# A state-space scan on one core: turned sums two units behind, and some inputs made by TensorE

## The reference, cut to what matters

```
x, z   = split(h @ in_proj)                  # 512 channels each
xc     = silu(conv4(x) + conv_b)             # 4 taps along time, per channel
dt, Bm, Cm = split(xc @ x_proj)              # 16 states
dt     = softplus(dt @ dt_proj + dt_b)
h[t]   = exp(dt[t] * A) * h[t-1] + dt[t] * xc[t] * Bm[t]    # per channel and state
y[t]   = sum over states of h[t] * Cm[t]
out    = ((y + D * xc) * silu(z)) @ out_proj
```

## Time and profile before

| | |
|---|---|
| median of 3 runs | 2810.18 us (2809.4 to 2818.44) |
| the profiled execution | 2800.64 us, span 2798.8 us |
| busy: TensorE, VectorE, ScalarE, GpSimd | 2379.9, 2118.9, 1563.2, 1135.3 us (85, 76, 56, 41%) |
| TensorE's granted clock, mean | 0.916 |
| stage A | 0 to about 520 us, scans from 44.76 us on |
| stage B | about 1515 to 2030 us |
| chain that ended last, by engine | TensorE 42%, VectorE 25%, ScalarE 11%, GpSimd 9% |

### The profile page before, as it was taken

One profiled execution on the slowest core, in us unless ns is written; L12 is line 12 of the kernel. 1 busy time (PEld: TensorE's weight loads), 2 busy tenths in 40 slices (PEclk: granted clock), 3 DMA queues, 4 the chain that ended last, 5 costly groups with the idle time before them and its releaser, 6 DMA issues.

```text
span 2798.8 us, 32693 instructions
## 1 busy us (share of the span) xinstructions
PE 2379.9 (85%) x11300; PEld 1600.5 (57%) x11300; DVE 2118.9 (76%) x3100; ACT 1563.2 (56%) x2734; POOL 1135.3 (41%) x829
## 2 busy tenths in 40 slices
PE   5989896689998798958995798897778987899998
PEld 2333432467776687847884234333333444799998
DVE  5999999699997365538894899999864653577776
ACT  6676574255665455516884866766313444266673
POOL 3889998200000444210221699989601134100004
PEclk9999999899999799979997899999867886799999
DMA  4032040570000000012421330303084231256553
GB/s 178 2 120 92 30 146 0 196 256 1 24 1 1 36 1 31 16 66 95 162 106 53 121 115 7 121 31 102 0 124 103 55 81 58 91 189 224 210 197 95
DMA packets 101607, 247.36 MB, mean 88 GB/s; under 512 B 9285, under 2 KB 65361, under 8 KB 94274
## 3 DMA queue, kind: packets, MB, share of 16 engines
q1 hardware_dynamic: 88530, 222.43, 24.6%
q0 software_dynamic: 5376, 14.70, 1.6%
q10 hardware_dynamic: 7536, 8.13, 1.2%
HBM read 187.96 MB, written 48.81 MB: 85 GB/s over the span
## 4 chain that ended last, share of the span: by engine, by line
PE 42%; DVE 25%; ACT 11%; issue 9%; POOL 9%; DMA 1%; SPq 1%; POOLq 1%; ACTq 1%; DVEq 0%
PE psum L111 7%; DVE psum L758 7%; PE psum L112 7%; PE psum L113 7%; PE psum L498 5%; POOL bu L372 4%; PE psum L118 3%; POOL ch L415 3%; ACT WH L3526 2%; ACT g L3673 2%; DVE ch L775 2%; PE psum L481 2%; DVE ch L758 2%; PE psum L2967 1%; PE psum L2895 1%
## 5 line engine op out<-in xcount | busy, mean ns | idle before, releaser
L372 POOL TENSOR_TENSOR bu<-u,row 128x1024 f32<-128x1024 f32 x254 | 594.8, 2354 | 137.0 <-DVE psum L758 47.5
L498 PE MATMUL psum<-ch,ident 128*128 128x512 f32 x1024 | 513.2, 634 | 114.6 <-DVE ch L775 63.7
L758 DVE TENSOR_TENSOR_SCAN psum<-psum,bu 128x1024 f32<-128x1024 f32 x210 | 479.8, 2285 | 22.1 <-ACT psum L590 21.2
L498 PEld LDWEIGHTS psum<-ch,ident 128*128 128x128 f32 x1024 | 190.4, 198 | 401.6 <-issue 184.1
L590 ACT ACTIVATE psum<-dt,A 128x511 f32<-128x511 f32 x512 | 332.1, 681 | 0.4
L775 DVE TENSOR_TENSOR ch<-psum,row 128x1024 f32<-128x1024 f32 x210 | 256.6, 1222 | 5.7
L3673 ACT ACTIVATE g<-psum,bias 128x256 f32<-128x256 f32 x248 | 101.1, 470 | 133.8 <-PE psum L113 129.6
L3495 POOL DMA_INDIRECT R<-m1res,gi x26 | 26.2, 1006 | 340.3 <-DMA m1res<-ob 324.2
L462 PE MATMUL psum<-hT,inw 128*128 128x512 f32 x256 | 130.0, 637 | 27.9 <-ACT xs L536 20.6
L111 PE MATMUL psum<-WH,hs 128*128 128x256 f32 x496 | 144.8, 292 | 5.0 <-DVE hs L3753 2.2
L111 PE MATMUL psum<-xT,WH 128*128 128x256 f32 x496 | 142.0, 286 | 7.6 <-DVE xT L3716 7.6
(11 more groups left out here) (456 smaller groups left out, 6536.7 us busy)
## 6 DMA issues: line engine op xcount, KB each, us to landing
W<-in_m1W SPq DMA_DIRECT2D x24, 2052.0 KB, 8.5
row<-Ascr SPq DMA_DIRECT2D x64, 512.0 KB, 5.7
...
```

Source lines behind the costliest of these rows:

```text
L372: e.tensor_tensor(m.bu[i % 3][:, :, :], u, m.row[:, g, 0, :, :], ALU.mult).then_inc(*m.fed.up)
L498: p = pe.matmul(m.y, k.ident, m.ch[i % RING_C][:, j, :], start=False, stop=g == UNITS - 1 and j == 1)
L758: dve.tensor_tensor_scan(to, flat, m.bu[i % 3][:, :, :].rearrange("p a n -> p (a n)"), 0.0, ALU.mult, ALU.add).then_inc(*m.scan.up)
```

## The change

TensorE's sum of unit i moves two slots later, to slot i + 2, and is made turned: each 128 x 128 block of h*C is the stationary operand and the identity moves, so y has time on the partitions. D*x is now a product of ScalarE (`mamba_direct_act`), turned into y in the same way. The gate is applied to turned y in unit 2 of a block, for which z is made with time on the partitions ("z by channel block"); the result is turned back by an item "yt" before the output projection. Unit 5 of every block gets its u*B from TensorE: u is turned (`mamba_turned_pe`), copied by ScalarE, and multiplied with diagonals of B which VectorE makes once per batch from an item "bt"; the decays of that unit go to an SBUF tile of their own. GpSimd makes the other seven, from three tiles counted over those units alone, and h*C of units 1, 3 and 5. Conv block 0 goes from GpSimd to TensorE. The slots of the items change, items of the batch ahead come before "out" in a slot, conv is drained in its own slot, the silu of z moves to slot 5 and that of xc to slot 16. The diagonals for conv are made in slots 8 and 9 of the first batch. Cut to its core:

```diff
+RING_B = 3
 RING_C = 4
 SIX = 6
+FROM_PE = (5,)
+BY_POOL = (1, 3)
...
-FIRST = [("h", 0), ("h", 1)] + [("in", i) for i in range(4)] + [("conv", 3), ("xp", 0)] + [("dt", i) for i in range(4)]
...
-BEFORE = {2: ("out", 0), 3: ("out", 1), 4: ("out", 2), 5: ("out", 3)}
-AHEAD = {6: ("h", 0), 7: ("h", 1), 8: ("in", 0), 9: ("in", 1), 11: ("in", 2), 12: ("in", 3),
-         14: ("conv", 1), 16: ("conv", 2), 18: ("conv", 3),
-         21: ("xp", 0), 22: ("dt", 0), 23: ("dt", 1), 24: ("dt", 2), 25: ("dt", 3),
-         26: ("z", 0), 28: ("z", 1), 29: ("z", 2), 30: ("z", 3)}
+FIRST = [("h", 0), ("h", 1)] + [("in", i) for i in range(4)] + [("conv", 3), ("xp", 0)] + [("dt", i) for i in range(4)] + [("bt", 0)]
...
+OPENING = {0: ("z", 0), 1: ("z", 1), 2: ("z", 2)}
+OWN = {3: ("z", 3), 13: ("yt", 0), 21: ("yt", 1), 28: ("yt", 2)}
+BEFORE = {4: ("yt", 3), 5: ("out", 0), 6: ("out", 1), 8: ("out", 2), 10: ("out", 3)}
+AHEAD = {6: ("h", 0), 7: ("h", 1), 8: ("in", 0), 9: ("in", 1), 10: ("in", 2), 11: ("in", 3),
+         12: ("conv", 0), 13: ("conv", 1), 14: ("conv", 2), 15: ("conv", 3),
+         17: ("xp", 0), 18: ("dt", 0), 19: ("dt", 1), 20: ("dt", 2), 22: ("dt", 3),
+         24: ("z", 0), 25: ("z", 1), 27: ("z", 2), 29: ("bt", 0)}
...
+    if s in OWN:
+        o.append((OWN[s][0], b, OWN[s][1]))
+    if b + 1 < B and s in AHEAD:
+        o.append((AHEAD[s][0], b + 1, AHEAD[s][1]))
     if b and s in BEFORE:
         o.append((BEFORE[s][0], b - 1, BEFORE[s][1]))
-    if b + 1 < B and s in AHEAD:
-        o.append((AHEAD[s][0], b + 1, AHEAD[s][1]))
...
-    b, n = i // PER, i % PER
-    return n % UNITS in (2, 5) and (b == B - 1 or n in (2, 5, 18, 21, 26))
+    return from_pe(i) or i % UNITS in BY_POOL
...
-            for j in range(2):
+            for j in (1,) if g in FROM_PE else range(2):
...
+def mamba_turned_pe(k, m, pe, i):
+
+    s = i // UNITS
+    pe.wait_ge(*m.u_in(s))
+    if i >= RING_A:
+        pe.wait_ge(*mamba_left(m, i - RING_A))
+    for c in range(4):
+        p = turn_in(k, pe, m.a[i % RING_A][:, 0, 128 * c:128 * c + 128], m.u[s % 2][:, 128 * c:128 * c + 128])
+    p.then_inc(*m.turned.up)
+
+
+def mamba_turned_act(k, m, act, s):
+    act.wait_ge(*m.turned(s))
+    act.copy(m.uT[:, :, :], m.a[(UNITS * s + FROM_PE[0]) % RING_A][:, 0, :].rearrange("p (c n) -> p c n", c=4)).then_inc(*m.uT_in.up)
+
+
+def mamba_input_pe(k, m, pe, i):
+
+    s, g = i // UNITS, i % UNITS
+    b, db = s // 4, s % 4
+    if g == FROM_PE[0]:
+        pe.wait_ge(*m.uT_in(s))
+    elif i >= RING_A:
+        pe.wait_ge(*mamba_left(m, i - RING_A))
+    if db == 0:
+        pe.wait_ge(*m.drawn(mamba_use("bt", b, 0)))
+    for j in range(2):
+        for c in range(4):
+            p = pe.matmul(m.a[i % RING_A][:, j, 128 * c:128 * c + 128], m.uT[:, c, :], m.diag_B[g][:, j, c, :], start=True, stop=True)
+    p.then_inc(*m.fed_pe.up)
...
+        if i + 2 < PER * B and not from_pe(i + 2):
             mamba_input(k, m, pool, i + 2)
         if by_pool(i):
             mamba_met_pool(k, m, pool, i)
-        if b + 1 < B and 9 <= n < 16:
-            mamba_conv_pool(k, m, pool, b + 1, n - 9)
...
-        if 28 <= n and b + 1 < B:
-            if n == 28:
+        if n == 0 and b:
+            mamba_dt(k, m, pool, 4 * b + 3)
+        if 29 <= n and b + 1 < B:
+            if n == 29:
...
+    elif w == "z":
+        for c in range(4):
+            for f in range(2):
+                p = pe.matmul(bank[:, 128 * c:128 * c + 128], m.hT[:, f, 128 * c:128 * c + 128], m.inw[:, f, T + 128 * j:T + 128 * j + 128],
+                              start=f == 0, stop=f == 1)
+    elif w == "yt":
+        pe.wait_ge(*m.gated(4 * b + j))
+        for c in range(4):
+            p = turn_in(k, pe, bank[:, 128 * c:128 * c + 128], m.yzT[:, c, :])
+    elif w == "bt":
+        pe.wait_ge(*m.drawn(mamba_use("xp", b, 0)))
+        W = R + 32
+        for c in range(4):
+            p = turn_in(k, pe, bank[:, W * c:W * c + W], m.xd[0:W, 128 * c:128 * c + 128])
...
-            p = pe.matmul(bank, m.dg[:, 4 * (j - 1) + f, :], m.xs[:, j, f:f + T], start=f == 0, stop=f == 3)
+            p = pe.matmul(bank, m.dg[:, 4 * (j - 1) + f, :] if j else m.dg0[:, f, :], m.xs[:, j, f:f + T], start=f == 0, stop=f == 3)
...
+def mamba_sum_pe(k, m, pe, i):
+
+    s, g = i // UNITS, i % UNITS
+    if g == 0:
+        if s:
+            pe.wait_ge(*m.gated(s - 1))
+        pe.wait_ge(*m.dx_in(s))
+        for c in range(4):
+            p = pe.matmul(m.y[:, c, :], m.dx[:, 128 * c:128 * c + 128], k.ident, start=c == 0, stop=False, is_transpose=True)
+        p.then_inc(*m.direct.up)
+    pe.wait_ge(*mamba_out(m, i))
+    for j in range(2):
+        for c in range(4):
+            p = pe.matmul(m.y[:, c, :], m.ch[i % RING_C][:, j, 128 * c:128 * c + 128], k.ident, start=False,
+                          stop=g == UNITS - 1 and j == 1 and c == 3, is_transpose=True)
+    p.then_inc(*m.summed.up)
...
-        s, g = i // UNITS, i % UNITS
+        if (i + 1) % UNITS == FROM_PE[0]:
+            mamba_input_pe(k, m, pe, i + 1)
         for item in mamba_items(i):
             mamba_item_pe(k, m, pe, *item)
-        if g == 0:
-            pe.wait_ge(*(m.gated(s - 1) if s else m.diag(1)))
-            pe.matmul(m.y, m.dg[:, 12 + s % 4, :], m.xc[:, s % SIX, :], start=True, stop=False).then_inc(*m.direct.up)
-        pe.wait_ge(*mamba_out(m, i))
-        for j in range(2):
-            p = pe.matmul(m.y, k.ident, m.ch[i % RING_C][:, j, :], start=False, stop=g == UNITS - 1 and j == 1)
-        p.then_inc(*m.summed.up)
+        if i >= 2:
+            mamba_sum_pe(k, m, pe, i - 2)
+        if (i + 2) % UNITS == FROM_PE[0]:
+            mamba_turned_pe(k, m, pe, i + 2)
+    for i in range(PER * B - 2, PER * B):
+        mamba_sum_pe(k, m, pe, i)
+    mamba_item_pe(k, m, pe, "yt", B - 1, 3)
...
+    elif w == "yt":
+        act.copy(m.yz[:, j, :], bank).then_inc(*m.drawn.up)
...
+        if b:
+            act.wait_ge(*m.gated(4 * (b - 1) + j))
+        act.copy(m.sz[:, j, :], bank).then_inc(*m.drawn.up)
...
-    for j in range(4):
-        z = m.sz[:, (4 * b + j) % SIX, :]
-        e = act.activation(z, z, ACT.Silu)
-    e.then_inc(*m.sz_in.up)
+    act.activation(m.sz[:, :, :], m.sz[:, :, :], ACT.Silu).then_inc(*m.sz_in.up)
+
+
+def mamba_direct_act(k, m, act, s):
+
+    act.wait_ge(*m.xc_in(s))
+    if s:
+        act.wait_ge(*m.direct(s - 1))
+    act.activation(m.dx[:, :], m.xc[:, s % SIX, :], ACT.Identity, scale=pv(k, m.L + "D", 4)[:, s % 4:s % 4 + 1]).then_inc(*m.dx_in.up)
...
+    if from_pe(i):
+        e = NTH[i]
+        if e:
+            act.wait_ge(*m.scan(FED_PE[e - 1]))
+        else:
+            act.wait_ge(*m.zeros(2))
+        a = m.ad[0]
+    else:
+        if i >= RING_A:
+            act.wait_ge(*mamba_left(m, i - RING_A))
+        a = m.a[i % RING_A]
+        act.copy(a[:, :, 0], m.zero[:, :])
...
+    mamba_direct_act(k, m, act, 0)
...
-
-        for item in mamba_items(i - 1) if i else []:
-            if item[0] == "conv":
-                mamba_item_act(k, m, act, *item)
+            if (i + 2) % UNITS == FROM_PE[0]:
+                mamba_turned_act(k, m, act, (i + 2) // UNITS)
         for item in mamba_items(i):
-            if item[0] != "conv":
-                mamba_item_act(k, m, act, *item)
+            mamba_item_act(k, m, act, *item)
...
-        if n == 6 and b:
+        if i in (8, 9):
+            for j in range(8) if i == 8 else range(4):
+                o, n0 = (m.dg, 4) if i == 8 else (m.dg0, 0)
+                g = act.activation(o[:, j, :], k.ident, ACT.Identity, scale=cw[:, n0 + j:n0 + j + 1])
+            g.then_inc(*m.diag.up)
+        if n == 14 and b:
             x_stats_act(k, act, 4 * (m.rnd + 1) + b - 1)
-        if n == (2 if b else 4):
+        if n == 5:
             mamba_gate_act(k, m, act, b)
-        if n == 5 and b + 1 < B:
+        if n == 4 and b + 1 < B:
             mamba_rows_act(k, m, act, b + 1)
-        if n == 19 and b + 1 < B:
+        if n % UNITS == 3 and i // UNITS + 1 < 4 * B:
+            mamba_direct_act(k, m, act, i // UNITS + 1)
+        if n == 16 and b + 1 < B:
             mamba_silu_act(k, m, act, b + 1)
-        if n in (24, 25) and b + 1 < B:
-            mamba_soft_exp_act(k, m, act, b + 1, 2 * (n - 24), 2 * (n - 24) + 2)
-        if n == 26 and b + 1 < B:
+        if n in (20, 22) and b + 1 < B:
+            mamba_soft_exp_act(k, m, act, b + 1, n - 20, n - 18)
+        if n == 23 and b + 1 < B:
             mamba_soft_log_act(k, m, act, 3 * b + 5, 0, 4)
...
-        if b:
-            dve.wait_ge(*m.full(mamba_use("out", b - 1, 3)))
-    dve.tensor_tensor(m.yz[:, db, :], m.y, m.sz[:, s % SIX, :], ALU.mult).then_inc(*m.gated.up)
+    if s:
+        dve.wait_ge(*m.full(mamba_use("yt", (s - 1) // 4, (s - 1) % 4)))
+    dve.tensor_tensor(m.yzT[:, :, :], m.y, m.sz[:, db, :].rearrange("p (c n) -> p c n", c=4), ALU.mult).then_inc(*m.gated.up)
...
+def mamba_diag_dve(k, m, dve, b, n):
+
...
```

(18 more changed lines are left out.)

134 lines of the change are left out of this document (64 added, 70 removed).

## The result

The changed kernel takes 2923.0 us (median of four runs, 2911.9 to 2928.7) against 2809.8: ratio 1.0392, interval 1.0354 to 1.0430. It is slower, as forecast, but by 113 us where 40 were forecast, and outside the range of 2785 to 2890.

A forecast was written before the change was run, and what follows sets the result against it. VectorE was taken to set the pace, GpSimd close behind. Per stage 6.2 + 10.7 + 10.4 - 6.5 - 0.4 = 20.4 us; two stages 40.8, rounded to +40 on 2810.2, gave 2850 us, range 2785 to 2890.

The forecast's parts named there:

- (a): Middle batch, units 3 to 8: VectorE waits 5.4 us for out1 behind h0, 0.4 for u*B; 6.0 with rounding.
- (b): Middle batch, units 8 to 13: out3, in3 and u*B of unit 13 come late, with the gate; 3.4 us.
- (c): Middle batch, units 13 to 21: serial conv, silu, xp, dt chain of 36.7 us against VectorE's 26.0; 10.6 us idle.
- (d): Middle batch, units 24 to 29: log delays a decay 2.2, gate waits 1.4, u*B of 29 0.3; 3.9 us.
- The first batch: First batch of a stage: first scan's wait for dt3 hidden by unit 2's decay; +6.2 us in all.
- The last batch: Last batch of a stage, nothing prepared ahead: 100.4 us to the last scan against 106.8; -6.5 us.
- the end: End of a stage: gate waits 1.1 us instead of 2.8, then a turned block and copy 1.3; -0.4 us.
- rival 3: TensorE's clock falls, slowing (c)'s matmuls: 2880 us if only early on, 2970 throughout; chance 0.10 shared with slow sums.
- the signs of being wrong: Middle batches under 112 us, VectorE's waits moving to GpSimd's inputs, or middle-batch clock below 0.9, blaming clock, not order.
- Rival 1: VectorE and GpSimd set the pace, ScalarE's chain being shorter: middle batches near 105, 2744 us; chance 0.20.
- a draw: Last-batch gains and partial stalls cancel: middle batch 116 to 118 us, total 2802 to 2818; chance 0.10.

The follow-up runs named there:

- the spread items: Changed kernel with the next batch's conv in slots 12, 14, 16, 18 and its later items moved along, to slot 30: 2874.0 us, ratio 1.0240.
- the pair of fillers: Plain or turned zero blocks before every sum, against the changed kernel with out blocks first and next batch's items spread: 2929.1 and 2931.2 us.
- the best order without u*B: Changed kernel without u*B on TensorE, out blocks in slots 5 to 8, in 9 to 12, conv 14, 15, 17, 18, log 27: 2799.7 us, ratio 0.9968.

## Why the prediction came out as it did

**Right.** VectorE's own work is 102.2 us a middle batch (101.2 forecast), GpSimd's 102.6 (103.6), a turned sum 1.03 to 1.09 us with its run-out at full clock (0.9). The stalls are mostly where they were laid, and their cause, the order of items on ScalarE and TensorE, is one of the two that the runs bear out; the other is u*B on TensorE. The scan of unit 21 came 39.8 us after that of 13 (36.7), and the busy time of sums fell from 513.2 to 293.1 us. VectorE's waits for decays were to grow and did not; those for TensorE did, to some 83 us a stage.

**Wrong: the size of nearly every stall.** The second batch step by step, as time less VectorE's own work in those units (by the spacing of the same units where nothing is late; the parts add up to 34.9 where the windows give 34.2):

| step | forecast | measured | what was missed |
|---|---|---|---|
| (a) units 3 to 8 | 6.0 | 10.2 | out1 ready 23.9 us after scan 3, not 19.5: out1 and z3 at half clock; on the way GpSimd's input 1.9 late at unit 4, u*B 1.6 at unit 5 |
| (b) 8 to 13 | 3.4 | 5.2 | u*B of unit 13 3.2 late (2.3 set), outs and gate 2.0 (1.1) |
| (c) 13 to 21 | 10.6 | 13.8 | xp at half clock, 6.35 where 3.6 was set |
| (d) 24 to 29 | 3.9 | 4.5 | |
| rest | 0 | 1.2 | GpSimd's input 0.95 late at unit 2 |

That is 136.4 (with the own work 1 us higher) in place of 125.1, and 133.3 in the third batch. The first batch: its first scan came 5.7 us later, where I had that hidden. VectorE's timeline:

```profile
49.30 1.22 DVE L798 TENSOR_TENSOR row<-ident,psum 128x1024 f32<-128x1024 f32 x1 [4.52 <-ACT xs L607]
50.44 2.29 DVE L865 TENSOR_TENSOR_SCAN psum<-psum,bu 128x1024 f32<-128x1024 f32 x1
```

The product that forms the diagonals of B waits for dt3's drain and stands in VectorE's line ahead of scan 0. I had it right that something waits for dt3, but hid it behind the decay of unit 2, which only unit 2 needs. Together with 6.0 us more in the batch that is 11.7 for the first batch where 6.2 was set. The last batch gained 3.0 and not 6.5, and the end lost 4.1 where it was to gain 0.4: with the granted clock at 0.79 in the last batch and 0.67 from its last scan to 575 us, the four closing out blocks took 10.2 us where they took 7.17. Against the forecast a stage is 33 us worse: 5.5 first, 19.5 middle, 3.5 last, 4.5 end.

**The steps that failed** are two prices. The mechanism was right; the sum had them too low.

**TensorE's pieces were priced at full clock**, from the faster of the rows. After the change TensorE has idle stretches ahead of out1, xp and z3, and its clock is at the lower level when these come: 1.9, 2.75 and 1.7 us more on the path of the second batch, 6.35 of the 11.3 by which it missed. In the third batch out1 is 1.8 and xp 1.7 longer, 3.5 of 8.2, and at the end of a stage the out blocks are 3.0 of the 4.5. By these rows the clock is some 13 of the 33 us a stage; the rest is waits, but for 2 us of VectorE's own work. I had the clock as rival 3, with idle between turned sums named for it, but inside (c) alone and at +5 a batch. One of the signs of being wrong did come, a granted clock of 0.87 in a middle batch, and it did not mean what I had laid down for it: at 0.86 the spread items were 43 us faster, and with out1 back at full clock (1.99 us) nothing was gained. That TensorE turns was not the reason either: the Trainium skill, "TensorE: Matmul & The Clock Gate", Part 4: PE-mode transpose, says that turning does not count as busy, and the pair of fillers contradicts it, 0.96 and 0.96. TensorE had waited before each of the slow blocks (5.2 us before out1, 4.3 before xp), and with fillers between the sums the clock was higher; no run took the waits away and left the rest as it was. How much of the 113 us is the lower clock alone stays open, since every run that raised the clock by 0.05 or more did it with more work in TensorE's line and was slower.

**u*B was under-priced.** It stood in the forecast as matmuls of 1.9 us and a copy of 0.59, with 0.4, part of 3.4 and 0.3 us of stall in a middle batch and nothing at the first scan. Without it the changed kernel is 57 us faster, though VectorE then has more to do. The copy waits in ScalarE's line and TensorE waits for the copy, so each is late by whatever the other has in front of it; ScalarE alone stood 19.4 us in the second batch for turned u. Without that hand-over, the matmuls kept, 42 of 53 us went. In the first stage 4.8 us are the later first scan (50.4 and 45.7 us).

Rival 1 (VectorE and GpSimd set the pace, middle batches near 105) came true in no run: the best order without u*B takes 113 us a middle batch, of which VectorE is busy 105, and as a time it is a draw.
